# Second attention with stacked single-pass scores, 72-column value blocks, and another spread of the experts' remainders

## The reference, cut to what matters

```python
# second attention: queries and keys from the normalised x, values from ctx
# 8 batches x 4 patches of 128 columns, 8 heads of 8 channels
q = Wq @ qp + bq ; k = Wk @ qp + bk ; val = Wv @ vp + bv        # (32 patches, 64, 128)
scores = einsum('bhdi,bhdj->bhij', qh, kh) / sqrt(8)
scores = where(mask > 0, scores, -1e9)
attn = softmax(scores) ; o = gelu(attn applied to val)
x = x + tanh(g_xattn[1]) * (Wo @ o + bo) * mask
# experts: top 2 of 8, each 512 x 512
y = mean over the two chosen experts of relu(x @ W_e + b_e)
x = x + tanh(g_ffn[1]) * y
```

## Time and profile before

| | us |
|---|---|
| median of 3 runs (1076.47 to 1077.78) | 1077.44 |
| the profiled execution's own time | 1079.99 |
| its span | 1078.2 |

### The profile page before, as it was taken

How to read it: one execution, slowest core, us unless ns; L and a number is a source line. 1 busy time by engine, 2 the same in 40 slices (tenths; PEclk the granted TensorE clock), 3 DMA queues, 4 the chain that set the end, 5 groups by cost and what they waited for, 6 DMA issues and landing times.

```text
span 1078.2 us, 14253 instructions
## 1 busy us (share of the span) xinstructions
PE 963.1 (89%) x4851; PEld 739.8 (69%) x4851; DVE 622.2 (58%) x1077; ACT 337.6 (31%) x599; POOL 411.5 (38%) x404
## 2 busy tenths in 40 slices
PE   4899999999998999999999988969999998757990
PEld 4677778877777877778778667737777675345770
DVE  5864764465752565753756655655555554958334
ACT  4322132132241141232231321125555456422220
POOL 3541522431620431521514234455433332527540
PEclk9899999999999999999999998979999996659996
DMA  8020210010200110200200203060000002223437
GB/s 288 11 79 1 66 41 11 28 51 30 76 3 12 40 40 30 78 1 11 78 1 1 70 1 97 1 243 11 15 16 10 0 1 95 108 78 117 140 129 259
DMA packets 37591, 63.77 MB, mean 59 GB/s; under 512 B 5600, under 2 KB 13216, under 8 KB 37408
## 3 DMA queue, kind: packets, MB, share of 16 engines
q1 hardware_dynamic: 32416, 50.70, 13.9%
q0 software_dynamic: 3680, 12.06, 3.4%
q10 hardware_dynamic: 1440, 0.24, 0.1%
HBM read 52.77 MB, written 10.22 MB: 58 GB/s over the span
## 4 chain that ended last, share of the span: by engine, by line
PE 81%; DVE 8%; issue 4%; ACT 2%; DMA 2%; POOL 2%; ACTq 1%; DVEq 0%; SPq 0%; POOLq 0%
PE ps L1289 17%; PE ps L1291 16%; PE ps L1290 16%; PE ps L1501 5%; PE ps L1378 5%; PE ps L1520 5%; PE ps L1386 4%; PE ps L1508 3%; PE ps L1394 2%; PE ps L1488 2%; DVE w_lo L1143 2%; PE ps L1570 1%; DVE at_lo L968 1%; PE ps L1299 1%; PE ps L1528 1%
## 5 line engine op out<-in xcount | busy, mean ns | idle before, releaser
L476 POOL TENSOR_TENSOR q_t<-rot_a,rot_b 128x512 f32<-128x512 f32 x64 | 82.5, 1288 | 147.9 <-DVE rot_b L893 147.9
L1289 PE MATMUL ps<-wo_hi,at_hi 128*128 128x512 f32 x256 | 109.2, 427 | 18.6 <-DVE at_lo L968 11.9
L891 DVE TENSOR_TENSOR rot_a<-ps,cos 128x512 f32<-128x512 f32 x80 | 55.3, 692 | 114.9 <-PE ps L1291 114.9
L543 POOL TENSOR_TENSOR k_blk<-k_raw,m_full 32x512 f32<-32x512 f32 x64 | 80.9, 1264 | 90.0 <-ACT k_raw L751 86.2
L1289 PE MATMUL ps<-xt_hi,wq_hi 128*128 128x512 f32 x256 | 108.2, 423 | 0.2 <-issue 0.2
L1291 PE MATMUL ps<-xt_hi,wq_lo 128*128 128x512 f32 x256 | 101.5, 396 | 0.0
L1290 PE MATMUL ps<-xt_lo,wq_hi 128*128 128x512 f32 x256 | 101.4, 396 | 0.0
L1291 PE MATMUL ps<-wo_hi,at_lo 128*128 128x512 f32 x256 | 100.8, 394 | 0.0
L1290 PE MATMUL ps<-wo_lo,at_hi 128*128 128x512 f32 x256 | 100.1, 391 | 0.0
L696 ACT ACTIVATE at_hi<-ps 128x512 fp32r<-128x512 f32 x64 | 38.2, 598 | 190.6 <-PE ps L1394 190.6
L973 DVE TENSOR_TENSOR X<-ps,X 128x512 f32<-128x512 f32 x64 | 44.3, 692 | 85.9 <-PE ps L1291 85.9
(11 more groups left out here) (219 smaller groups left out, 2195.0 us busy)
## 6 DMA issues: line engine op xcount, KB each, us to landing
wq_raw<-in_wq SPq DMA_DIRECT2D x8, 1024.0 KB, 5.5
wo_raw<-in_wo SPq DMA_DIRECT2D x8, 1024.0 KB, 5.3
w_raw<-in_we SPq DMA_DIRECT2D x8, 1024.0 KB, 9.5
y_in<-y_rows SPq DMA_DIRECT2D x16, 256.0 KB, 5.4
X<-in_x SPq DMA_DIRECT2D x4, 512.0 KB, 13.0
wk_raw<-in_wk SPq DMA_DIRECT2D x8, 256.0 KB, 2.8
q_t<-in_ctx_t SPq DMA_DIRECT2D x2, 1024.0 KB, 10.5
wv_raw<-in_wv SPq DMA_DIRECT2D x4, 512.0 KB, 4.6
```

The lines of the kernel that those rows point to most:

```text
L476: nc.gpsimd.tensor_tensor(dst, rot_a[:, r % 2, :], rot_b[:, r % 2, :], ALU.add).then_inc(rope_ok, 1)
L543: last = nc.gpsimd.tensor_tensor(k_blk[part, j, grp, :, hd, :], heads(k_raw[part, grp, :]), heads(m_full[part, j, :]), ALU.mult)
L891: nc.vector.tensor_tensor(heads(rot_a[:, r % 2, :]), heads(bank), bcast(cos[:, :], 4), ALU.mult)
L1289: nc.tensor.matmul(dst, w_hi, x_hi, start=start and k == 0, stop=False)
```

## The change

Queries and keys now come from one matmul of 512 columns (`wqk1`), evicted once by DVE (`evict`, with bias and mask factor) into `qk_raw`. It is split into `qk_hi` (ACT, `round_qk`) and `qk_lo` (POOL, `remainder`). SP then copies rows of the two within SBUF so that rounded part and remainder stand stacked on the partitions (`k3`: high, low, high; `q3`: high, high, low), with a 97th row for the mask. One `fp32r` matmul over 97 partitions (`scores`) gives the same three-term product. These are 14 small copies a batch. POOL still spreads the keys, now 96 partitions at a time. The values lie as blocks of 72 columns (64 channels and 8 sums) in a padded tile, and the eight heads of a patch add up in one such block of PSUM. The projections run two batches ahead, those of batches 0 and 1 within the first feed-forward. The loops over batches are unrolled. FIRST goes from 6 to 4, and the experts are loaded one a batch. Remainders: expert 0 by DVE and expert 2 by POOL within the output loop, expert 1 by DVE and expert 3 by POOL after it, and 16 parts during the tiles (DVE 9, POOL 7).

```diff
+            def stack(b):                                   # SP
+                j = b % 2
+                half = HG * DH
+                sp.wait_ge(qkl_ok, CREDIT + b + 1)
+                if b >= 1:
+                    sp.wait_ge(kb_ok, CREDIT + H1 * b)
+                for g in range(2):
+                    rows = slice(E1 + g * half, E1 + (g + 1) * half)
+                    for n, part in enumerate((qk_hi, qk_lo, qk_hi)):
+                        sp.dma_start(k3[n * half:(n + 1) * half, g, :].bitcast(F32), part[rows, :].bitcast(F32)).then_inc(k3_in[g], 16)
+                if b == 0:
+                    sp.wait_ge(pen_ok, CREDIT + 3)
+                if b >= 2:
+                    sp.wait_ge(s2_mm, CREDIT + H1 * (b - 1))
+                for g in range(2):
+                    rows = slice(g * half, (g + 1) * half)
+                    for n, part in enumerate((qk_hi, qk_hi, qk_lo)):
+                        sp.dma_start(q3[n * half:(n + 1) * half, j, g, :].bitcast(F32), part[rows, :].bitcast(F32)).then_inc(q3_in[j], 16)
+                    sp.dma_start(k_blk[PARTS:PARTS + 1, j, g, :, :, :].bitcast(F32),
+                                 pen[b:b + 1, :, :, :]).then_inc(pen_in[j], 16)
+
+            stack(0)
+            stack(1)
             sp.wait_ge(x2_ok, CREDIT + B)
-            for e in range(FIRST):
-                load_expert(e)
             for b in range(2, B):
-                sp.wait_ge(pq_mm, CREDIT + 5 * (b - 1))
+                stack(b)
+                sp.wait_ge(vc_mm, CREDIT + b - 1)
                 load_ctx(b, b % 2)
+                if b - 2 < FIRST:
+                    load_expert(b - 2)
...
+            def remainder(b):                               # POOL
+                gp.wait_ge(qkh_ok, CREDIT + b + 1)
+                lo_part(qk_lo[:, :], qk_raw[:, :], qk_hi[:, :], qkl_ok)
+            def keys(b):
+                for u in range(H1):
+                    patch, g = divmod(u, 2)
+                    if u < 2:
+                        gp.wait_ge(k3_in[g], 48 * b + 48)
+                    if b >= 2:
+                        gp.wait_ge(s2_mm, CREDIT + H1 * (b - 2) + u + 1)
+                    nc.gpsimd.tensor_tensor(k_blk[0:PARTS, b % 2, g, patch, :, :], ...
+            remainder(1)
+            for b in range(B):
+                keys(b)
+                if b + 2 < B:
+                    remainder(b + 2)
...
+            def round_qk(b):                                # ACT
+                ac.wait_ge(qk_ev, CREDIT + b + 1)
+                if b >= 1:
+                    for g in range(2):
+                        ac.wait_ge(k3_in[g], 48 * b)
+                    ac.wait_ge(q3_in[1 - b % 2], 48 * (b + b % 2))
+                hi_part(qk_hi[:, :], qk_raw[:, :], qkh_ok)
...
                         turned(b - 1, H1 - 1)
                     if u == 4 and not first:
                         out_turned(b - 1, 1 - j)
-                    if not last and 2 <= u <= 5:
-                        proj_out(b + 1, 1 - j, u - 2)
+                    if more and u == 3:
+                        round_qk(b + 2)
...
+            def context(b, j):                              # PE
+                pe.wait_ge(cv_ok, CREDIT + b)
+                pe.wait_ge(ctxs_in[j], 8 * (b - j) + 16)
+                for a in range(PATCH):
+                    last = nc.tensor.matmul(ps[:, 1, a * E1:(a + 1) * E1], ctx_s[:, j, a * P:(a + 1) * P], wv1[:, :], start=True, stop=True)
+                last.then_inc(vc_mm, 1)
...
                     elif not last:
                         scores(b + 1, 1 - j, u + 2 - H1)
-                    if not last and 1 <= u <= 5:
-                        proj(b + 1, 1 - j, u - 1)
+                    if more and u == 1:
+                        pe.wait_ge(qk_ev, CREDIT + b + 2)
+                        proj(b + 2, j, h, 0)
+                    if not last and u == 3:
+                        context(b + 1, 1 - j)
                     if u >= 1:
                         turn(b, u - 1)
...
             mix(0, 0, first=True)                           # DVE, first feed-forward
             mix(1, 1)
+            nc.vector.memset(q3[PARTS:PARTS + 1, :, :, :].bitcast(F32), 1.0).then_inc(pen_ok, 1)
+            nc.vector.tensor_scalar(mask_8[:, :], mask_8[:, :], 0.0, MASKED, ALU.is_gt, ALU.mult).then_inc(pen_ok, 1)
+            nc.vector.tensor_scalar(pen[:, :, :, :], ...  # 8 x 2048
             for b in range(2, B):
                 mix(b, b % 2, last=b == B - 1)
                 row_stats(2, b - 2, b % 2, x2_ok)
+                if b == B - 3:
+                    rows(0, 0, p_w)
+                    kept(0, 0)
+                if b == B - 2:
+                    evict(0, 0, 7)
+                    rows(1, 1, p_w)
+                    kept(1, 1)
+            evict(1, 1, 7)
...
                 turned(2, b - 3, (b - 3) % 2)               # DVE, output loop
+                if b - 3 < KT:
+                    expert_lo(b - 3)
...
-                for n in range(3 * KT + 3 * i, min(3 * KT + 3 * i + 2, EX * KT)):
-                    expert_lo(n)
+                if i < EX - 1:                              # DVE, tiles
+                    expert_lo(4 * KT + 2 * i)
+                if i == EX - 3 or i == EX - 2:
+                    expert_lo(4 * KT + i + 9)
```

More of the change, by code:

```diff
@@ L760, in out_turned, with batch @@
                 nc.scalar.activation(o_t[:, b, :], ps[0:E1, 6 + j, :], ACT.Copy).then_inc(ot_ev, 1)
-            def batch(b, j, first=False, last=False):
+            def batch(b, j, first=False, more=True):
                 for u in range(H1):
@@ L772, in batch @@
                         out_turned(b - 1, 1 - j)
-                    if not last and 2 <= u <= 5:
-                        proj_out(b + 1, 1 - j, u - 2)
-            for n in range(4):
-                proj_out(0, 0, n)
+                    if more and u == 3:
+                        round_qk(b + 2)
             batch(0, 0, first=True)
-            with ac.Fori(0, (B - 2) // 2) as i:
-                batch(2 * i + 1, 1)
-                batch(2 * i + 2, 0)
-            batch(B - 1, 1, last=True)
+            for b in range(1, B):
+                batch(b, b % 2, more=b + 2 < B)
             turned(B - 1, H1 - 1)
@@ L1045, in first_rows @@
                 normalise(b, j, h_ok)
-            first_rows(0, 0)
-            first_rows(1, 1)
-            mix_lo(0, 0)
-            mix(0, 0, first=True)
-            mix(1, 1)
-            for b in range(2, B):
-                mix(b, b % 2, last=b == B - 1)
-                row_stats(2, b - 2, b % 2, x2_ok)
-            def rows(b, j):
-                ve.wait_ge(rstd_ok, CREDIT + B * 2 + b + 1)
-                normalise(b, j, hc_ok)
-                nc.vector.tensor_scalar(m_mul[:, j, :], mask_bb[:, b, :], 0.0, aug[:, 0:1], ALU.is_gt, ALU.mult).then_inc(mm_ok, 1)
@@ L1117, in _ @@
             batch(0, 0, first=True)
-            with ve.Fori(0, (B - 2) // 2) as i:
-                batch(2 * i + 1, 1)
-                batch(2 * i + 2, 0)
-            batch(B - 1, 1, last=True)
+            for b in range(1, B):
+                batch(b, b % 2, more=b + 2 < B, last=b == B - 1)
             over_sums(B - 1, 1)
@@ L1465, in mix, with proj @@
                     lora_out(b - 1, 1 - j)
+            def proj(b, j, rows, bank):
+                pe.wait_ge(hc_ok, CREDIT + b + 1)
+                nc.tensor.matmul(ps[:, bank, :], wqk1[:, :], rows[:, j, :], start=True, stop=True).then_inc(qk_mm, 1)
             turn_rows(1, 0, 0, 0)
             mix(0, 0, first=True)
-            with pe.Fori(0, (B - 2) // 2) as i:
-                mix(2 * i + 1, 1)
-                mix(2 * i + 2, 0)
-            mix(B - 1, 1, last=True)
+            for b in range(1, B):
+                mix(b, b % 2, last=b == B - 1)
+                if b >= B - 2:
+                    pe.wait_ge(qk_ev, CREDIT + b - B + 2)
+                    proj(b - B + 2, b % 2, p_w, 7)
@@ L1530, in turn_out, with batch @@
                 last.then_inc(ot_mm, 1)
-            def batch(b, j, first=False, last=False):
+            def batch(b, j, first=False, more=True, last=False):
                 for u in range(H1):
@@ L1550, in batch @@
                         turn_out(b - 1, 1 - j)
-            for n in range(5):
-                proj(0, 0, n)
+            context(0, 0)
             scores(0, 0, 0)
@@ L1611, in _ @@
                 last = nc.tensor.matmul(ps[:, 2, b * EX:64], ones_r[:, :], sel[:, 0:B - b, :], start=False, stop=b == B - 1)
-            last.then_inc(pre_mm, 1)
+            last.then_inc(rank_mm, 1)
             for n in range(B * TOP):
@@ L1626, in parts_done @@
             def parts_done(i):
-                behind = range(3 * KT, (i + 1) * KT)
-                in_loop = sum(n % 3 == 2 for n in behind)
-                return min(i + 1, 2) * KT + len(behind) - in_loop, (KT if i >= 2 else 0) + in_loop
+                if i < 4:
+                    return min(i + 1, 2) * KT, max(i - 1, 0) * KT
```

(3 more changed lines are left out.)

317 lines of the change are left out of this document (156 added, 161 removed).

## The result

The changed kernel takes 1085.43 us (median of 6 runs, 1083.71 to 1088.93); the kernel before took 1077.16 beside it (1076.19 to 1082.04). The ratio is 1.0075, with a 95% interval of 1.0058 to 1.0092: 8.3 us slower, where 9.4 were forecast. The profiled execution has a span of 1083.4 us.

The account below looks back on a forecast made before the run. A loop of waits through SP's copies, the late context load, PE, ACT and POOL was taken to bound the second attention. Span 1078.2 + 8.6 (attention) + 0.8 (behind it) = 1087.6 us; median 1077.44 + 9.4, about 1087, range 1044 to 1104.

Parts of the forecast that it names:

- The ring: Second attention: copies, context load, PE, ACT's rounding, POOL's remainder and keys form a loop of 25.7 us a batch; chance 0.52.
- step 1: SP's queue, second attention: 14 copies at 0.51 us each, then the context load, issued 7.05 us after the keys, landing 2.7 later.
- K: The moment in the second attention when POOL has finished the keys of the batch before, keys(b - 1).
- Step 2: PE, second attention: stops some 6 us for the context's load, then values 1.8 us and transposes 1.1 at the lower clock.
- Steps 3 and 4: Second attention: ACT's turned copy before rounding, 1.15 us with handover; POOL's next remainder, 1.3 us, ahead of the keys.
- Step 4: POOL, second attention: the next remainder, 1.3 us, stands ahead of the keys, whose eight parts take 10.54 us.
- The sums of 72 columns: PE's weighted sums in the second attention: 0.1 us more a unit, bounds 0 and +0.2.
- The rival of the low clock: Second attention: PE's light unit never regains full clock, about 31 us a batch; up to 1134 us in all; chance 0.09.
- The feed-forward: First feed-forward, DVE: three mask-row operations cost +2.5 us (1 to 3.5); other additions nothing, up to +2.
- Behind the attention: Output loop and tiles: respread remainders cost +4.1 us in the loop and return 3.3 in the tiles, sum +0.8.
- Short issues: SP's copies, second attention: at 0.37 us each a round is 23.8 us, 1074 us in all; chance 0.18.
- looser ring: Second attention: context load doesn't end PE's wait, a round is 20.6 us, 1052 in all; chance 0.14 shared with PE's pace.

Follow-up runs that it names:

- both_nine: Against the kernel with context load ahead of copies and keys ahead of the next remainder: weighted sums multiply 9 columns instead of 72; 1104.54 us.
- both_old_spread: Against the kernel with context load and keys both moved ahead: experts' remainders spread over DVE and POOL as before the change; 1027.36 us.
- ctx_first: Against the changed kernel: SP issues the load of ctx_s ahead of the 14 copies instead of behind them; 1051.51 us, ratio 0.9767.
- both edits: Against the changed kernel: context load ahead of the copies, and POOL's keys ahead of the next remainder; 1028.86 us.
- the last two variants: With old remainder spread: mask operations spread over mixes of batches 1, 2, 3, 1026.11 us; then also batches 0 and 1's mask-row copies ahead of stacks, 1026.05 us.
- both_first: Against the changed kernel: context load ahead of the copies, and POOL's keys ahead of the next remainder; 1028.86 us, ratio 0.9562.
- four_more: Against the changed kernel: four more unused copies in each stack from batch 2 on, ahead of the context's load; 1101.46 us, ratio 1.0226.

## Why the prediction was right, step by step

The time, the sign and the mechanism held: 1087 against 1085.4. The profiled execution after reached the first routing sum 3.7 us earlier than the one before, in a part that the change hardly touches; in the kernels of the experiments that sum lies between 650.3 and 653.9, so most of it is spread between executions. The routing sums of before, then of after:

```profile
L1021 DVE TENSOR_TENSOR lg<-ps,route_bias x8: 142/175/175, 654.7 to 693.8; 128x16 f32<-128x16 f32 x8
```

```profile
L1059 DVE TENSOR_TENSOR lg<-ps,route_bias x8: 154/174/175, 651.0 to 693.3; 128x16 f32<-128x16 f32 x8
```

So landmarks are counted from that sum (the forecast's from 654.7, the measured ones from 651.0), and the two spans differ by 5.2 us where the medians differ by 8.3.

| | forecast | measured |
|---|---|---|
| remainder 0 done | 44.7 | 43.7 |
| keys 0 done | 65.3 | 63.8 |
| context 2 | 95.7 | 96.1 |
| context 7 | 224.2 | 221.2 |
| attention ends | 256.6 | 254.7 |
| from there to the end | 176.3 | 177.7 |

- **The ring, step 1, the copies.** SP issues one each 0.63 us, not 0.51: the load comes at K + 8.86 instead of K + 7.05, +1.8. I had priced copies within SBUF by a row of eight loads from HBM; my upper bound was 0.6. That the source makes the difference isn't shown: the load from HBM behind the copies holds SP for 0.58 us too (819.75). The landing took 3.08 with the semaphore instead of 2.7.
- **Step 2, PE.** Its waits ahead of the context were forecast at some 6 us each (5 to 8); they are 3.1, 3.9, 6.2, 3.6, none and 8.0. Values 1.73 (forecast 1.8), turn 1.10 (1.1), at the lower clock as forecast in all places but one: the values at 848.54 took 1.00 us and waited for nothing. PE itself had been busy for 24.9 of the 25.7 us up to them, at a mean clock of 0.62, so in that round it was PE and not the ring that came last. The rule of the Trainium skill that the prediction weighed ("TensorE: Matmul & The Clock Gate", "HAM oscillation — how this bites in real kernels") held in the rounds with a wait.
- **Steps 3 and 4, ACT and POOL's remainder.** 1.19 and 1.23 (1.3 and 1.3).
- **Step 4, the keys.** The mis-sized term: eight parts take 8.02 us (8.2 to 8.4 in three batches), not 10.54, so 1.00 a part instead of 1.32. I had carried the price over from a row with another shape and allowed a tenth; it was a quarter. That it came out is luck in part: -2.5 here and +2.2 in the copies and the landing cancel. The rounds are 25.0 us (contexts 747.08 to 872.21, five rounds) against 25.7.
- **The sums of 72 columns.** Forecast +0.1 us a unit; measured nothing. The rival of the low clock was right to fear a light unit: it named the scores of 512 columns and the 72-column sums as reasons against it, and both_nine shows that the scores alone don't keep the full clock.
- **The feed-forward.** The three mask operations were to cost 2.5 and the rest nothing, up to 2; together they cost 3.1 (routing sums over 42.24 us instead of 39.13). The gaps between the sums divide it: 1.8 at the mask operations (12.7 us instead of 10.9 from the second sum to the fourth), 1.5 at the rows and evictions (12.2 instead of 10.7 from the sixth to the eighth).
- **Behind the attention.** Loop +4.1 and tiles -3.3, sum +0.8, were forecast; both_old_spread shows 2.9, -2.1 and 0.8. The stage as a whole is 2.2 longer than before (177.7 against 175.5). Of the other 1.4, about 1 lies between the kernel before and those with the old spread, behind the output loop: from the last `xt_lo` to the end of the span the kernel before takes 144.0 us, the kernels with the old spread 145.0 to 145.1. What makes it wasn't traced.
- **Short issues, looser ring.** Neither: the copies cost 0.63, and ctx_first shows that the load ended the wait. The 20.6 us of a looser ring is what ctx_first has (20.0 to 21.1), and its 1051.5 us that rival's 1052. Of the 35 us that the rival took off, though, the prediction's terms give only 27 (five rounds of 5 and 1.8 of the context); the rest stands there without a working.

The change was worth more than its result: single-pass scores make a batch on PE 16.4 us instead of 23.5, as computed, and the order of instructions on two queues ate it. With both edits and the old spread of remainders the kernel takes 1027.4 us, 4.8% less than the kernel before; the last two variants can't be told from it.

## What to carry to other kernels

When a change lightens the bounding engine, follow one batch around every queue before adding up what the engine saves: a load that could have gone long ago doesn't belong behind copies that wait for the last result, and work for this batch belongs ahead of preparation for the next. Look at the granted clock before making PE's work smaller: here leaving out columns that take PE no time of their own cost over 70 us.

## What was not expected of the hardware

- Matmuls against 128 x 128 weights of 9 and of 72 columns have the same pitch (0.10 us each at full clock, 0.20 at the lower one), but beside the same single-pass scores a PE busy for all of 100 us stayed at 1.2 GHz with the narrow ones (both_nine), and one busy for 95.47 of them at 2.4 GHz with the wide ones (both_first).
- Behind its waits for the context PE worked without a gap for 5 to 20 us before the full clock came back (0.50 from 822.80 to 842.50, busy 19.67 of 19.70 us).
- A copy of 32 x 512 within SBUF holds SP for 0.59 us and the next starts 0.63 after it; in a ring it cost 0.67 (four_more).
- POOL takes 8.02 us for eight multiplications of 96 x 512 with a broadcast operand, where eight four-head parts of before, 32 x 512, took 10.54. Which of shape, start partition or broadcast does it wasn't tried.
